# Fourth steps that begin with four query products, last rows loaded tile by tile, and other orders in the first units and at the end

## The reference

```python
q, k, v = x @ W0q.T + b0q, ctx @ W0k.T + b0k, ctx @ W0v.T + b0v
x = softmax(where(mask == 0, -1e9, q @ k.T)) @ v + x              # layer 0
Q, K, V = heads(x @ W1q.T + bq), heads(ctx @ W1k.T + bk), heads(ctx @ W1v.T + bv)
c = softmax(Q @ K.T / sqrt(32)) @ V                               # layer 1, 16 heads
x = c @ Wo.T + bo + x
out = (x - mean(x)) / sqrt(var(x) + 1e-5) * gamma + beta
```

## Time and profile before

| | us |
|---|---|
| median of 3 runs | 389.39 |
| lowest and highest | 385.28, 391.73 |
| the profiled execution | 386.4 |
| its span | 384.6 |
| TensorE busy in it | 364.7 |
| VectorE, ScalarE, GpSimd busy | 258.9, 252.9, 225.6 |
| TensorE's granted clock, mean share | 0.984 |

### The profile page before, as it was taken

One profiled execution on the slowest core, in us unless ns is written; L12 is line 12 of the kernel. 1 busy time (PEld: TensorE's weight loads), 2 busy tenths in 40 slices (PEclk: granted clock), 3 DMA queues, 4 the chain that ended last, 5 costly groups with the idle time before them and its releaser, 6 DMA issues.

```text
span 384.6 us, 17162 instructions
## 1 busy us (share of the span) xinstructions
PE 364.7 (95%) x7288; PEld 282.5 (73%) x7288; DVE 258.9 (67%) x591; ACT 252.9 (66%) x1190; POOL 225.6 (59%) x248
## 2 busy tenths in 40 slices
PE   8999999899999999999999999999999997999893
PEld 7978875677767777777777777777777775777572
DVE  0245558477678768676867686877787784668686
ACT  1423797667757875877587777797677755767520
POOL 0520276444543987388827885588638872767752
PEclk9999999899999999999999999999999998999989
DMA  8943742500140222304240325032413005030213
GB/s 293 396 156 92 270 100 81 190 5 3 58 132 16 99 98 72 104 30 140 77 126 12 109 79 172 4 112 87 124 50 112 30 19 193 18 123 8 80 51 115
DMA packets 19063, 38.82 MB, mean 101 GB/s; under 512 B 2190, under 2 KB 3726, under 8 KB 18859
## 3 DMA queue, kind: packets, MB, share of 16 engines
q1 hardware_dynamic: 18447, 37.03, 29.2%
q10 hardware_dynamic: 540, 0.69, 0.6%
HBM read 26.49 MB, written 8.39 MB: 91 GB/s over the span
## 4 chain that ended last, share of the span: by engine, by line
PE 61%; DVE 13%; ACT 13%; issue 5%; POOL 3%; DMA 3%; SPq 2%; DVEq 0%; ACTq 0%
PE ps_qo L1149 18%; PE ps_qo L1238 14%; ACT prob L612 12%; PE ps_mid L1177 9%; PE ps_qo L1101 4%; PE ps_mid L1165 4%; DVE pt L835 3%; PE ps_mid L1064 2%; DVE nb L885 2%; PE ps_hi L1165 2%; PE ps_mid L1077 2%; SPq L355 1%; DVE x_raw L1046 1%; PE ps_hi L1064 1%; DMA raw<-in_w0k 1%
## 5 line engine op out<-in xcount | busy, mean ns | idle before, releaser
L454 POOL TENSOR_TENSOR prob<-prob,rc 128x308 f32<-128x308 f32 x128 | 92.5, 724 | 109.3 <-DVE rc L842 108.2
L612 ACT ACTIVATE prob<-ps_mid,mx 128x77 f32<-128x77 f32 x256 | 78.8, 334 | 30.3 <-DVE mx L823 30.3
L612 ACT ACTIVATE prob<-ps_hi,mx 128x77 f32<-128x77 f32 x256 | 80.0, 380 | 0.0
L835 DVE STREAM_TRANSPOSE pt<-prob 128x768 f32<-128x768 f32 x64 | 61.8, 967 | 8.0 <-PE ps_mid L1177 4.4
L612 ACT ACTIVATION_READ_ACCUMULATOR prob<-ps_hi,mx 128x1 f32 x256 | 67.1, 262 | 0.0
L612 ACT ACTIVATION_READ_ACCUMULATOR prob<-ps_mid,mx 128x1 f32 x256 | 54.9, 214 | 0.0
L1149 PE MATMUL ps_qo<-x_h,wq_h 128*128 128x512 f32 x128 | 54.0, 422 | 0.2 <-DMA u_b<-rest 0.2
L823 DVE TENSOR_REDUCE mx<-ps_mid 128x4 f32<-128x308 f32 x64 | 27.5, 471 | 37.8 <-PE ps_hi L1165 37.8
L1149 PE MATMUL ps_qo<-x_h,wq_l 128*128 128x512 f32 x128 | 52.6, 411 | 0.0
L842 DVE RECIPROCAL rc<-sm 128x4 f32<-128x4 f32 x128 | 22.1, 172 | 43.1 <-ACT prob L612 42.7
L1177 PE MATMUL ps_mid<-pt,v 32*32 32x128 f32 (+1 forms) x2976 | 48.6, 278 | 1.9 <-DVE p_b L764 1.0
(11 more groups left out here) (133 smaller groups left out, 688.2 us busy)
## 6 DMA issues: line engine op xcount, KB each, us to landing
x_raw<-in_xT SPq DMA_DIRECT2D x14, 512.0 KB, 3.9
y<-in_x SPq DMA_DIRECT2D x28, 256.0 KB, 4.6
out<-y SPq DMA_DIRECT2D x28, 256.0 KB, 2.1
mask_sb<-in_mask SPq DMA_DIRECT2D x8, 154.0 KB, 2.6
raw<-in_w0q SPq DMA_DIRECT2D x4, 256.0 KB, 5.7
x_raw<-in_xT SPq DMA_DIRECT2D x1, 1024.0 KB, 7.9
raw<-in_w0v SPq DMA_DIRECT2D x1, 1024.0 KB, 10.1
raw<-in_w1q SPq DMA_DIRECT2D x1, 1024.0 KB, 12.2
```

The lines of the kernel that those rows point to most:

```text
L454: nc.gpsimd.tensor_tensor(ap, ap, wide(rc[:, k % 2, h], KEYS), ALU.mult).then_inc(prob_done, 1)
L612: e = nc.scalar.activation(prob[:, k % 2, t, h, 0:KEYS], ps_s[h][:, t * KEYS:(t + 1) * KEYS], ACT.Exp, bias=mx[:, k % 2, h, t:t + 1], accu ...
L835: nc.vector.transpose(pt[:, own].rearrange("p h n t r -> p t (h n) r"), prob[:, k % 2, :, own].rearrange("p t h (n r) -> p t (h n) r", r=Q ...
```

## The change

Six edits; the arithmetic stays:

1. In units with g = 3 the first four query products of the next unit stand ahead of the first two output products and the transposes. ScalarE does `round_p0` behind the exponentials of head 0, not ahead of all.
2. The 1 MB load of the last block's rows in unit 27 becomes four loads of 256 KB, two in unit 29 and two in unit 30, each behind the scores of its unit, with a semaphore for each tile.
3. In units 2 and 3 the 14 query products are cut: 10 ahead of the context (in unit 2 four of them ahead of the transposes), the last 4 between its halves. The wait for the stacked weights `u_stacked[1]`, which stood ahead of all query products of unit 3, now stands ahead of the last four.
4. On GpSimd `affine` of tile 3 of block 5 moves from unit 30 to 29, and that of tile 1 of block 6 from ahead of unit 31's `scale_probs` to behind them.
5. At the end `gamma` and `beta` of tile 3 of block 6 wait until VectorE has done `last_beta` of tile 0 and of tile 1.
6. The store of the last block's tile 1 stands ahead of that of block 6's tile 3.

```diff
-        ld_last = sem("ld_last")
+        ld_last = [sem(f"ld_last{t}") for t in range(TILES)]
...
+            def load_last(k, t):
+
+                sp.wait_ge(s_done, k + 1)
+                sp.dma_start(last_y[:, t], x[LAST % 2, TILES * (LAST // 2) + t]).then_inc(ld_last[t], 16)
...
-                if g == 3 and b == LAST - 1:
+                if g == 1 and b == LAST:
                     sp.wait_ge(xl_ready, CH * BLOCKS)
                     sp.wait_ge(xh_ready, CH * BLOCKS)
-                    last_x = x[LAST % 2, TILES * (LAST // 2):TILES * (LAST // 2 + 1)]
-                    sp.dma_start(last_y[:], last_x.rearrange("t p d -> p t d")).then_inc(ld_last, 16)
+                    load_last(k, 0)
+                    load_last(k, 1)
+                if g == 2 and b == LAST:
+                    load_last(k, 2)
+                    load_last(k, 3)
...
             store_last(0)
+            store_last(1)
             store(0, LAST - 1, 3)
-            store_last(1)
...
                 if k == UNITS - 1:
                     affine(i, b - 1, 0)
-                    affine(i, b - 1, 1)
...
+                if g == 1 and b == LAST:
+                    affine(i, b - 2, 3)
                 if g == 2:
                     root(i, b - 1, 0)
                     x_rest(i, b + 1, 2)
                     x_rest(i, b + 1, 3)
+                if g == 2 and b < LAST:
                     affine(i, b - 2, 3)
...
                 root(0, LAST - 1, 1)
+                affine(0, LAST - 1, 1)
                 affine(0, LAST - 1, 2)
                 last_root(0)
+                pool.wait_ge(last_beta_done, 1)
                 gamma(0, LAST - 1, 3)
                 last_root(1)
+                pool.wait_ge(last_beta_done, 2)
                 beta(0, LAST - 1, 3)
...
-                if g == 3:
-                    round_p0(i, b + 1)
                 for h in range(GROUP_HEADS):
                     exps(i, k, h)
+                    if g == 3 and h == 0:
+                        round_p0(i, b + 1)
...
                 if k == 2:
                     pe.wait_ge(add0_done, 2)
                     fold(1, 0, CH)
+                    query(0, k + 1, 0, 4)
                     transpose0(0, 1)
-                    query(0, k + 1, 0, QUERY)
+                    query(0, k + 1, 4, 10)
                 if k == 3:
-                    query(0, k + 1, 0, QUERY)
+                    query(0, k + 1, 0, 10)
                 if k > 0:
                     context_half(k - 1, 0)
+                if k > 1:
+                    query(0, k + 1, 10, QUERY)
+                if k > 0:
                     context_half(k - 1, 1)
...
                 else:
+                    query(i, k + 1, 0, 4)
                     part(0)
                     transpose0(i, b + 1)
-                    query(i, k + 1, 0, 5)
+                    query(i, k + 1, 4, 9)
                     part(1)
-                    query(i, k + 1, 5, 9)
                     context(i, k - 1)
```

More of the change, by code:

```diff
@@ L1021, in last_residual @@
                 dve.wait_ge(last_open, t + 1)
-                dve.wait_ge(ld_last, 16)
+                dve.wait_ge(ld_last[t], 16)
                 nc.vector.tensor_tensor(last_out[t][:], last_out[t][:], last_y[:, t], ALU.add).then_inc(last_added, 1)
```

## The result

| us | before | after |
|---|---|---|
| median | 389.94 (4 runs) | 377.22 (4 runs) |
| lowest and highest | 385.28, 391.73 | 373.1, 382.77 |
| profiled execution, its span | 386.4, 384.6 | 373.1, 371.3 |
| granted clock in it | 0.984 | 0.998 |

The ratio is 0.9676 with an interval of [0.9611, 0.974]: faster. The median is 377.22 where 375.5 was forecast. A second comparison of the same two kernels gave 0.9742 [0.9694, 0.979]. (The ratios leave disturbed executions out, one of 1118 us in the last experiment among them, and so need not be the quotient of the medians.)

The account below looks back on a forecast made before the run. TensorE, busy 364.7 of 384.6 us, was taken as the bound, except at the end (GpSimd and VectorE). Terms 4.5 + 3.6 + 1.0 + 3.0 = 12.1 us gave 374.3 or 377.3; 375.5 was taken, range 370.5 to 384.

Parts of the forecast that it names:

- Edit 1: Six units with g = 3: TensorE's waits for L858 (3.6 us) and L764 (1.0) go; 4.5 us taken.
- 4.6 the upper bound: Six units with g = 3: all 3.6 + 1.0 us of waits gone, TensorE then having no pause left.
- the price of the two waits: Unit 27: 0.59 us waiting for L858 at the output product, 0.16 us behind L764 at the context.
- Edit 2: Scores of unit 28: the 2.13 us pause and 1.54 us of low clock behind it go, 3.67 together; 3.6 taken.
- the pause moves to unit 29: Rival: two last tiles behind two y loads, again 1 MB in a row, make TensorE's instructions late there; 379.1 us, chance 0.17.
- another cause: Rival: unit 28's pause is not from the load, and the pauses in units 3 and 4 stay too; 380.1 us, chance 0.08.
- Edit 3: Units 3 and 4: both score pauses go, a new wait for VectorE's second transposition comes; 1.0 us taken, bounds -0.5 to 2.0.
- unit 4's pause: If unit 3's pause goes, the scores of unit 4 begin at 75.8 and run without their 0.82 us pause.
- The end: Unit 31 to the end: 1.5 us from earlier scaling plus 1.86 from L1046 less 0.4 for roots, 3.0 us; bounds 1.5 to 3.9.
- the second transposition starts at 361.2 instead of 363.22 ... 2.0 us for all that follows: Unit 31: GpSimd's head products follow ScalarE, so context, last output products and root come 2.0 us earlier.
- 1.86 - 0.4 of L1046: End: two slow L1046 passes each lose 0.93 us when GpSimd's passes move away; roots of tiles 1 and 2 held about 0.2 each.
- a delay to GpSimd's next root: End: two affines behind GpSimd's root delay the root of the last block's tile 0 to 369.7, cutting 2.0 us to 1.5.

Follow-up runs that it names:

- edit 1 alone: Kernel before with only the new order of the fourth steps on TensorE and ScalarE's rounding of p_a behind head 0's exponentials: 377.54 us, ratio 0.9728.
- the half edit: Kernel before with only TensorE's new order of the fourth steps; ScalarE's round_p0 stays ahead of the exponentials: median 390.66 us, ratio 1.001.
- edit 2 alone: Kernel before with the last 512 rows loaded in four parts in units 29 and 30, not one 1 MB load in unit 27: 384.33 us, ratio 0.9871.
- without edit 2: Kernel after with block 6's tile 1 affine ahead of GpSimd's root, and the last rows again one 1 MB load in unit 27: 373.68 us, ratio 0.9654.
- edit 3 alone: Kernel before with only the query products of units 1 to 3 reordered: 388.9 us, ratio 1.0013.
- edits 4 to 6 alone: Kernel before with only GpSimd's affines moved, the last stores' order changed, and gamma and beta held back at the end: 389.86 us, ratio 1.0001.
- the load 4 us earlier: Affine ahead of GpSimd's root, last rows one 1 MB load, now issued in unit 27 ahead of the moves of p_a: 374.77 us, ratio 0.9665.
- the affine ahead of the root: Kernel after with block 6's tile 1 affine ahead of GpSimd's root of the last tiles, gamma between heads 2 and 3: 373.77 us, ratio 0.9675.

## Why the prediction was right, and where not

The number was right: 377.22 for 375.5. That it came so close is in part luck. The terms add up to 12.1 us and the edits gave 10.6 in the traces; edit 1 was taken 1.3 us too small, the end 1.9 and edit 3 some 0.5 too large, and these misses partly cancel. Of the terms:

- **Edit 1** was right in mechanism, and too small: 0.75 us a block predicted, 0.9 to 1.2 measured (edit 1 alone). I had called 4.6 the upper bound, "as TensorE then has no pause left". The term that was mis-sized is the price of the two waits, which I took from the idle times 0.59 and 0.16. A listed idle time begins at the end of the product ahead, but products follow one another every 0.233 us and each takes 0.39, so a product that waits could have begun before that end. From start to start, in unit 15 and counted from its maxima, the first product came at -0.55 us instead of 0.13 and the context at 4.03 instead of 4.95: 0.68 for the first wait, 0.24 for the second, 0.92 together, and 0.90 to 0.93 in all six blocks. What is left, 0 to 0.3 us a block, lies in the scores of the next unit, which took up to 0.35 us longer in the trace of before (unit 12); why, I have not found. That the context behind L764 is next in line, and that ScalarE's half is what keeps it off, is shown by the half edit.
- **Edit 2**: pause, low clock and price were right, 3.63 for 3.67. The step that failed is whose gain it is: the term stood beside edit 1's as if edit 2 were needed for it. I had looked at where the load comes, and not at whether the same fetch still meets it once the instructions ahead of it are 4 us early. Edit 1 alone removes the pause, edit 2 alone removes it, and taking edit 2 away changes nothing. The sum held since the 3.6 us were counted once and came once. Two small waits in units 29 and 30, 0.6 us for `ct_l` and 0.4 for `prob`, were not forecast. They are not the loads' either: edit 1 alone and the kernel without edit 2 have them too (0.5 or 0.6, and 0.4). The one for `ct_l` is in the ten traces without the pause of unit 28 and in none of the four with it.
- **The rival "the pause moves to unit 29"** did not happen: 512 KB behind two `y` loads left no pause. **The rival "another cause"** is settled by the traces. In all fourteen I looked at TensorE's pauses of 0.25 us or more without a releaser, from 38 us on: 39 of them. Counted by the matmuls that the program has issued before them, they stand at twelve places only, the same whatever the kernel: 726, 980, 1105, 2249, 2883, 3772, 4661, 4916, 5550, 5805, 6439 and 6567. The distances are 125 to 128 or a multiple of about 127, and 57 fetches for 7288 matmuls are one for each 128. Each pause ends 1.1 to 1.6 us after the latest fetch has landed. So these pauses are waits for the next 16 KB of instructions. The one of unit 28 has 6439 before it and waits for the 50th fetch. In seven of the fourteen traces that fetch begins within 0.1 us of the 6356th matmul; I take this as the time at which it is due. Measured from there, in us:

| trace | 1 MB load issued before that | 50th fetch late by | pause at unit 28 |
|---|---|---|---|
| edit 3 alone | 2.2 | 3.4 | 1.70 |
| TensorE's half | 2.2 | 3.8 | 1.86 |
| before | 2.2 | 3.9 | 2.13 |
| edits 4 to 6 alone | 2.2 | 4.3 | 2.56 |
| edit 1 alone; without edit 2 | 1.0 | 0.1; 0.0 | none |
| the load 4 us earlier | 5.2 | 0.1 | none |
| the seven without the 1 MB load | | 0.0 to 1.4 | none |

  In the four with a pause the DMA engines were 0.92 to 1.01 busy from the time at which the fetch was due until it began, and the pause is the delay less 1.7 to 1.9 us. This also explains the failed attempt to bring it back: that load came 3 us too early and was nearly through, so the engines, 0.94 busy in the 2 us ahead, did not hold the fetch. The Trainium skill's sentence ("Runtime: NRT & Kernel Launch", section Instruction fetch mechanics) that the fetch is hidden does not agree with these traces; by it edit 2 alone would have given nothing, where it gave 1.3%. What stays open is what else can make a fetch late: the 1.55 us of the half edit (the place 6567) came with idle DMA engines.
- **Edit 3**: 1.0 predicted, 0.45 in the trace, 0 in the times. Step by step: unit 3's pause went (right in the main: none of 0.25 us or more in six of eight traces with the edit, 0.35 and 0.45 in two; 0.41 to 1.16 in the six without it), TensorE waits for `pt` (right; 2.00 us, more than the pause gave, since the products that covered it now come behind it, so that unit 4 is only 0.45 us earlier), unit 4's pause stayed (wrong). It varies from execution to execution in either order: from none to 1.17 us in the eight traces with the edit, from none to 1.57 in the six without. The 0.45 is no more than that spread: three other traces with edit 3 and a full clock up to unit 5 stand at 0.18 earlier, 0.29 and 0.91 later than before.
- **The end**: 3.0 predicted, 1.1 measured. Behind `ct_l` the kernel after needs 15.11 us, before 16.48: 1.37, close to the 1.86 - 0.4 of L1046 (now L1059). The failed step is the first, "the second transposition starts at 361.2 instead of 363.22 ... 2.0 us for all that follows". Against unit 31's maxima the second transposition came 0.80 earlier. The first waits until the context of unit 30 has freed `pt`, and the reciprocal of head 3, which I had put at about 5.7 us behind the maxima, stands behind it in VectorE's queue and came at 6.8; head 3's product and the second transposition follow from that. And behind it 1.07 us are lost where I saw nothing: GpSimd's moved affine starts at 353.52, at once behind its root, beside VectorE's offset. With the affine put elsewhere the end is 27.78 to 27.81 us behind unit 31's maxima in five traces. With it behind the root it is 28.85 and 28.86 in two, and 30.44 and 30.46 in the two whose clock was low there. I had priced the affines as a delay to GpSimd's next root, which was not late (359.18, the last pass right behind it).
- **The first 2.7 us** of the difference I could not have forecast, and they are no gain.

What all this leaves: edit 1 carries nearly everything (ratio 0.9728 alone; 0.9676 and 0.9742 for all six). The best versions here are the kernel after with the affine ahead of the root, with or without edits 2 and 3 (0.9638 to 0.9675, each with an interval of about 0.005 to either side); these runs can't rank them. Of edit 1's 2.7%, 3.6 us or 0.9% are the pause, which edit 2 removes as well.

## What to carry to other kernels

Work that covers a wait on one engine often moves what another engine waits for: move both, and test the halves, for here half of the change was worth 0 and the whole 2.7%, the pause of unit 28 included. Terms of a sum that come from one and the same pause are not to be added: ask of each edit whether it would remove the pause by itself. Before a wait is put down to the engine that comes late, look for the buffer that its consumer must free first, here `pt` for the transposition, and for what stands ahead in the same queue. Price a wait from start to start and not by the idle time alone. And where an engine stops with nothing that releases it, count its instructions up to the stop: a count that is the same in other orders and other executions points at the fetch.

## What was not expected of the hardware

- A [128 x 2] operation of VectorE (the offset `nb`) took 1.23 us while GpSimd ran a [128 x 512] pass that had started 0.07 us before it, and 0.16 without one beside it: 1.23 in all four traces with the affine behind the root, 0.16 in the ten others. It ended when the pass ended. The same operation at the start of unit 31 shows it again: in the five traces in which a pass had begun 0.86 us before it, it took 0.45 or 0.46 and ended with the pass; in the nine others it took 0.12. This operation pays the rest of the other engine's pass. Not each small one does: a reciprocal of [128 x 4] took 0.18 us in the midst of a pass (356.54 in the kernel before).

```profile
353.01 0.45 DVE L885 SCALAR_TENSOR_TENSOR nb<-mv,rs 128x2 f32<-128x2 f32 x1
```

- TensorE's granted clock fell to half in the first units in all traces but four (after, the affine ahead, without edit 2, the early load), for 3 to 10 us at a time; the time of one kernel follows it, 373.1 us at a mean of 0.998 and 378.17 at 0.984. With the same instructions and the same wait of 2.00 us for `pt` one execution of the kernel after had it and another had not, so what decides is not in these rows; nor does each pause bring it (1.86 and 1.55 us in unit 28 of the half edit, clock 1.00 behind both).
